# Attention and feed-forward kernel: another order of the work on the first four tiles, and the scales' floor by an instruction with two tensors

## The chip, the cores and the metric

The kernel runs on one core of one Trainium2 chip. The metric is the device time of one execution in microseconds (us), lower is better. A core has five engines with an instruction queue each: TensorE (PE in the profile, its weight loads PEld), VectorE (DVE), ScalarE (ACT), GpSimd (POOL) and SyncE (SP, which only issues transfers here). Each engine takes its own instructions in program order and waits on semaphores that others raise.

## What is computed

```python
x = x + xattn(layernorm(x), ctx, ctx)      # x, ctx: 32 x 64 x 512, fp32
x = x + ffn(layernorm(x))

# xattn, for each batch entry: q = Wq x + bq, k = Wk ctx + bk, v = Wv ctx + bv  (64 x 64 weights)
#   8 heads of 64 columns: p = softmax(q k^T / 8), out = Wo (p v) + bo
# ffn: gate, up: 512 x 1792, down: 1792 x 512, int32 weights, one zero and one scale for 128 rows each
#   w = (imatrix - zero) * scale
#   y = (silu(x @ gate) * (x @ up)) @ down
```

## The kernel before

The 32 x 64 rows of `x` are 16 tiles of 128 rows (two batch entries each), and 4 chunks of 4 tiles. For each tile the attention has a fixed series of steps, and every engine has a few of them:

- `stats(0, t)` (VectorE), `rstd` (GpSimd, a power of -0.5), `shift` (VectorE) and `norm1` (ScalarE) make the first layer norm.
- `project(t)` (TensorE, line 663) makes q and k of both entries in PSUM; `take_qk(t, 0)` and `take_qk(t, 1)` (VectorE, L943) add the biases and put them into SBUF. Their buffer `qkT` is single, so `take_qk(t+1)` waits for `score(t)`.
- `score(t)` (TensorE, L673) makes the scores. `most(t)` (VectorE, L957) takes the largest one of each row, `less_max(t)` (L963) subtracts it, `power_of(t)` (ScalarE, L526) takes the exponential, `invert(t)` (VectorE, L970 and L973) makes the sum and its reciprocal, and `weigh(t)` (GpSimd, L391) multiplies by it.
- `values(t)` (TensorE, L681) and `take_v(t)` (ScalarE, L521) make v; `mix(t)` (TensorE, L692) applies Wo to the weights p, `take_a(t)` (ScalarE, L535) takes the result, `apply(t)` (TensorE, L703) multiplies by v, and `residual(t)` (VectorE, L982) adds it to `x`.
- `stats(1, t)`, `rstd`, `shift(1, t)`, `norm2(t)`, then `turn_x(t)` (TensorE, L722): the second layer norm, transposed. `take_x` (ScalarE, L544) and `rest_x` (VectorE, L989) split it into a high and a low part in `xT`. For the fourth tile this is done in halves (L616, L885, L621, L1119).

`PRE` is 4: the first four tiles go through all of this ahead of the loop over the feed-forward. I call this part the front; its order is written out by hand, as one list of calls for each engine. PSUM banks, `xn`, `v_sb` and `e_sb` are shared by neighbouring tiles, so a list sets which tile waits for which. `stir(n)` (TensorE, L796) is filler: n multiplications of the identity whose result nobody reads.

After the front comes a loop of places `q`, in which TensorE makes the gate and up products (`gate_up`, L764 and L766) and the down products (`down`, L777 and L778) of a chunk while the attention of the next tiles is put between them. `project`, `values` and `score` of the fifth tile (t = 4) reach into the loop: `project(4)` is still in the front, its `take_qk(4, 0)` and `take_qk(4, 1)` stand at the end of VectorE's front, and `score(4)` comes after the first `gate_up`. The start of the first `gate_up` waits for the low part of the fourth tile's first half (`s_lastlo`).

Two kinds of work stand beside the attention in the front. The int32 weights come in pieces of 512 KB with their zeros (SyncE waits for each of the first five pairs before it issues the next), and GpSimd's `less_zeros(k)` (L409) subtracts the zeros of a piece, `convert(k)` (ScalarE, L548) makes it a float. In the loop VectorE does both for every second piece (L997). And the scales are prepared once: ScalarE copies them from PSUM (L583, L584), VectorE's `prepare` (L1003 to L1010) takes the absolute values, their largest one in each column, a floor from it (`fl`) and a comparison with it, GpSimd's `raised` (L434) spreads the floor, VectorE's `divide` (L1016, L1019) puts in the scales that are above it and inverts, and GpSimd's `ratios` (L439 to L442) makes the ratios with which ScalarE rescales.

## Time and profile before

| | |
|---|---|
| time, median of 3 runs | 434.78 us (434.33 to 435.92) |
| the profiled execution's own time | 434.57 us |
| its span, first to last instruction | 432.8 us |
| mean granted TensorE clock in the span | 0.996 of 2.4 GHz |
| busy: PE, PEld, DVE, ACT, POOL | 410.4, 317.9, 330.4, 330.5, 265.8 us |
| start of the first `gate_up` (end of the front) | 45.45 us |
| PE busy in 0 to 46 us | 38.5 of 46 us, much of it filler |
| HBM read, written | 30.56 MB, 4.19 MB |

The span is one execution recorded by the hardware profiler; all times of instructions below count from its start. The profiled execution took 0.2 us less than the median. Busy time of an engine is not the same as being needed: each engine waits for others in the front, and TensorE fills its waits with `stir`.

### The profile page before, as it was taken

Reading aid. Unit: us, or ns where it says so; the run is one execution under the profiler, and the core shown is the slowest. Engines: PE = TensorE matmul, PEld = TensorE weight load, DVE = VectorE, ACT = ScalarE, POOL = GpSimd, SP = SyncE. Lnnn points to the kernel's source line nnn. Section 1 sums busy time; section 2 is a strip of 40 time slices with the busy share of each in tenths; the row PEclk is TensorE's granted clock in tenths of the full one; section 3 lists DMA queues with packets and bytes.
Section 4 is the critical chain, followed back from the end, with each engine's and each line's share of the span. In section 5 each row is a group of like instructions: output and inputs, shape, how many; then the busy total and the mean of one; then the engine's idle time right before and its main releaser. Section 6 shows DMA issues by size and latency. Waiting matters only on the chain.

```text
span 432.8 us, 10751 instructions
## 1 busy us (share of the span) xinstructions
PE 410.4 (95%) x4228; PEld 317.9 (73%) x4228; DVE 330.4 (76%) x582; ACT 330.5 (76%) x540; POOL 265.8 (61%) x264
## 2 busy tenths in 40 slices
PE   7878988999988999999999999999999999999994
PEld 5655666777856777777777878677877888888872
DVE  4778666998878778788887777787887667667676
ACT  2438898897877788687778888687888998988970
POOL 3335797899588654665473954755566555555561
PEclk9899999999999999999999999999999999999999
DMA  7677746966742000002010000000000000001003
GB/s 255 190 230 259 279 147 226 300 204 209 241 121 69 2 11 16 26 2 76 12 39 26 2 0 27 27 2 26 26 27 0 2 1 9 17 24 50 1 1 97
DMA packets 26792, 35.44 MB, mean 82 GB/s; under 512 B 1870, under 2 KB 18422, under 8 KB 26742
## 3 DMA queue, kind: packets, MB, share of 16 engines
q1 hardware_dynamic: 26434, 34.71, 24.5%
q8 instruction: 33, 0.54, 0.5%
q14 instruction: 17, 0.14, 0.1%
q10 hardware_dynamic: 244, 0.05, 0.1%
q0 software_dynamic: 64, 0.00, 0.0%
HBM read 30.56 MB, written 4.19 MB: 80 GB/s over the span
## 4 chain that ended last, share of the span: by engine, by line
PE 73%; DVE 9%; issue 6%; POOL 6%; ACT 4%; DMA 1%; POOLq 0%; SPq 0%; DVEq 0%; ACTq 0%
PE banks L764 20%; PE banks L766 19%; PE banks L777 10%; PE banks L778 9%; PE banks L663 4%; DVE yT L1039 2%; PE banks L703 2%; ACT banks L555 2%; PE banks L692 2%; PE banks L673 2%; PE banks L681 2%; POOL t_sb L416 1%; DVE st L925 1%; PE banks L722 1%; DVE qkT L943 1%
## 5 line engine op out<-in xcount | busy, mean ns | idle before, releaser
L555 ACT ACTIVATE banks<-banks,ratio 128x512 f32<-128x512 f32 x336 | 207.8, 664 | 34.9 <-PE banks L766 25.4
L1039 DVE SCALAR_TENSOR_TENSOR yT<-banks,sd,yT 128x512 f32<-128x512 f32 x208 | 154.1, 746 | 48.8 <-PE banks L778 48.1
L764 PE MATMUL banks<-xT,wgu 128*128 128x512 f32 x448 | 182.2, 407 | 5.2 <-DVE t_sb L1024 2.5
L766 PE MATMUL banks<-xT,wgu 128*128 128x512 f32 x448 | 175.1, 391 | 0.0
L416 POOL TENSOR_TENSOR t_sb<-t_sb,u_sb 128x512 f32<-128x512 f32 x56 | 72.7, 1298 | 63.1 <-DVE t_sb L1024 63.0
L764 PEld LDWEIGHTS banks<-xT,wgu 128*128 128x128 f32 x448 | 84.1, 188 | 27.6 <-issue 3.7
L766 PEld LDWEIGHTS banks<-xT,wgu 128*128 128x128 f32 x448 | 84.3, 188 | 15.2
L777 PE MATMUL banks<-hr,wd 128*128 128x512 f32 x224 | 89.3, 399 | 4.2 <-DVE yT L1039 2.3
L778 PE MATMUL banks<-hr,wd 128*128 128x512 f32 x224 | 87.5, 390 | 0.0
L429 POOL TENSOR_TENSOR hr<-t_sb,hr 128x512 fp32r<-128x512 f32 x56 | 73.1, 1305 | 5.1 <-ACT hr L577 0.7
L777 PEld LDWEIGHTS banks<-hr,wd 128*128 128x128 f32 x224 | 42.0, 188 | 19.3 <-DVE yT L1039 9.5
L1024 DVE SCALAR_TENSOR_TENSOR t_sb<-t_sb,banks 128x512 f32<-128x512 f32 x56 | 38.3, 684 | 20.5 <-ACT t_sb L563 20.4
L563 ACT ACTIVATE t_sb<-banks,half_g 128x512 f32<-128x512 f32 x56 | 38.9, 694 | 13.7 <-PE banks L766 10.1
L778 PEld LDWEIGHTS banks<-hr,wd 128*128 128x128 f32 x224 | 42.1, 188 | 8.1
L385 POOL TENSOR_TENSOR rs<-ve,power 128x1 f32<-128x1 f32 x32 | 18.9, 592 | 35.2 <-DVE ve L929 35.1
L571 ACT ACTIVATE u_sb<-banks,last_u 128x512 f32<-128x512 f32 x56 | 38.5, 688 | 0.9 <-POOL t_sb L416 0.9
L425 POOL CAST hr<-t_sb 128x512 fp32r<-128x512 f32 x55 | 35.0, 636 | 6.1 <-PE banks L778 3.0
L391 POOL TENSOR_TENSOR e_sb<-e_sb,ri 128x512 f32<-128x512 f32 x16 | 17.0, 1065 | 28.5 <-DVE ri L973 28.5
L925 DVE BATCH_NORM_STATS2 st<-x_sb 128x6 f32<-128x512 f32 x32 | 21.8, 681 | 3.6 <-DMA x_sb<-in_x 3.6
L521 ACT ACTIVATE v_sb<-banks,bvo 128x512 f32<-128x512 f32 x16 | 11.0, 687 | 15.8 <-PE banks L681 15.4
L409 POOL TENSOR_TENSOR wgu_in<-wgu_in,z_in 128x1024 int32<-128x1024 int32 x9 | 21.5, 2393 | 1.1 <-DMA z_in<-in_L_ffn_gate_z 1.1
L943 DVE TENSOR_TENSOR qkT<-banks,bqk 128x512 f32<-128x512 f32 x32 | 21.5, 679 | 0.8 <-PE banks L663 0.8
(93 smaller groups left out, 383.9 us busy)
## 6 DMA issues: line engine op xcount, KB each, us to landing
x_sb<-in_x SPq DMA_DIRECT2D x16, 256.0 KB, 5.2
out<-x_sb SPq DMA_DIRECT2D x16, 256.0 KB, 2.1
wgu_in<-in_L_ffn_gate_w SPq DMA_DIRECT2D x7, 512.0 KB, 5.7
z_in<-in_L_ffn_gate_z SPq DMA_DIRECT2D x7, 512.0 KB, 5.4
wgu_in<-in_L_ffn_up_w SPq DMA_DIRECT2D x7, 512.0 KB, 5.5
z_in<-in_L_ffn_up_z SPq DMA_DIRECT2D x7, 512.0 KB, 5.0
wd_in<-in_L_ffn_down_w SPq DMA_DIRECT2D x7, 512.0 KB, 5.3
z_in<-in_L_ffn_down_z SPq DMA_DIRECT2D x7, 512.0 KB, 4.6
```

The costliest lines, as they stand in the source:

```text
L416: pool.tensor_tensor(h, h, u_sb[:, :], ALU.mult).then_inc(s_h, 1)
L425: pool.tensor_copy(hr[:, n % 2, 0, :], t_sb[:, n % 2, :]).then_inc(s_hi, 1)
L429: pool.tensor_tensor(hr[:, n % 2, 1, :], t_sb[:, n % 2, :], hr[:, n % 2, 0, :].bitcast(F32), ALU.subtract).then_inc(s_lo, 1)
L555: act.activation(banks[:, bank, :], banks[:, bank, :], ACT.Copy, scale=ratio[:, m, g, it:it + 1]).then_inc(done[n % 2], 1)
L563: act.activation(t_sb[:, n % 2, :], banks[:, G_BANK[n % 2], :], ACT.Tanh, scale=half_g[:, it:it + 1]).then_inc(s_tanh, 1)
L571: act.activation(u_sb[:, :], banks[:, U_BANK[n % 2], :], ACT.Copy, scale=last_u[:, it:it + 1]).then_inc(s_uf, 1)
L764: pe.matmul(banks[:, bank, :], w, xT[:, c % 2, 0, g, :], start=g == 0, stop=False, skip_group_check=True)
L766: pe.matmul(banks[:, bank, :], w, xT[:, c % 2, 1, g, :], start=False, stop=True, skip_group_check=True).then_inc(full[n % 2], 1)
L777: pe.matmul(bank, w, hr[:, n % 2, 0, :], start=True, stop=False)
L778: pe.matmul(bank, w, hr[:, n % 2, 1, :], start=False, stop=True).then_inc(s_full, 1)
L1024: dve.scalar_tensor_tensor(t, t, 1.0, banks[:, G_BANK[n % 2], :], ALU.add, ALU.mult).then_inc(s_gt, 1)
L1039: dve.scalar_tensor_tensor(y, bank, sd[:, it, b:b + 1], y, ALU.mult, ALU.add).then_inc(s_free, 1)
```

## The change

Nothing of what is computed changes except the way in which one small step is written. The change has these parts:

1. VectorE: `take_qk(1, 0)` and `take_qk(1, 1)` stand together in front of `invert(0)`, and so do those of the third tile in front of the second tile's sum; `shift(0, t)` comes right after its statistics; `prepare()` stands behind `take_qk(2, 1)`, `most(1)` and `less_max(1)` ahead of it; `residual(2)` stands ahead of `invert(3)`, `divide()` moves up in front of `residual(2)`; both `take_qk(4, .)` stand at the very end. `rest_x(0)` comes after `invert(3)`.
2. TensorE: `score(1)`, `score(2)` and `score(3)` come sooner, ahead of `project(2)`, `project(3)` and `values(2)`; `turn_x(1)` moves behind `mix(3)`; the fillers are cut up otherwise.
3. ScalarE and GpSimd lists are put in a matching order: the copies of the scales after `take_v(0)`, `raised()` after `weigh(2)`, and `less_zeros(2)` before `weigh(3)` instead of behind it.
4. `invert(t)` waits for `weigh(t-1)` for t = 1, 2 and 3, not for 3 alone (the buffer of reciprocals is single).
5. The floor `max(fl * 2^-30, 1e-37)` is a `scalar_tensor_tensor` with a second tensor `tiny` (a column of 1e-37 that GpSimd sets) in place of a `tensor_scalar` with two constants.

```diff
+            pool.memset(tiny[:, :], 1e-37).then_inc(s_id, 1)
...
             weigh(0)
             less_zeros(0)
-            raised()
             weigh(1)
             rstd(1, 0)
             less_zeros(1)
             weigh(2)
+            raised()
             rstd(1, 1)
+            less_zeros(2)
             weigh(3)
-            less_zeros(2)
...
             mm.then_inc(s_tr2, 1)
-            stir(2)
+            stir(3)
+            pe.wait_ge(s_sub, 1)
+            score(1)
             pe.wait_ge(s_qk, 4)
             project(2)
             pe.wait_ge(s_wT, 3)
             values(0)
-            stir(1)
-            pe.wait_ge(s_sub, 1)
-            score(1)
+            stir(2)
...
             apply(2)
-            stir(2)
+            stir(3)
             pe.wait_ge(s_x1, 3)
             values(3)
-            turn_x(1)
-            stir(1)
+            stir(4)
             pe.wait_ge(s_v, 4)
             mix(3)
+            turn_x(1)
+            apply(3)
...
-                if t == PRE - 1:
+                if 1 <= t < PRE:
                     dve.wait_ge(s_p, t)
...
-                dve.tensor_scalar(fl[:, :, :], fl[:, :, :], 2.0 ** -30, 1e-37, ALU.mult, ALU.max).then_inc(s_pr, 1)
+                dve.wait_ge(s_id, 5)
+                dve.scalar_tensor_tensor(fl[:, :, :], fl[:, :, :], 2.0 ** -30,
+                                         tiny[:, :].unsqueeze(2).to_broadcast([P, 2, NI]), ALU.mult, ALU.max).then_inc(s_pr, 1)
...
             take_qk(1, 0)
+            take_qk(1, 1)
+            invert(0)
             take_w(1)
             dve.tensor_copy(bvo[:, :], banks[:, 7, 4 * D:4 * D + 2]).then_inc(s_wT, 1)
-            invert(0)
-            take_qk(1, 1)
-            shift(0, 3)
+            most(1)
+            take_qk(2, 0)
+            less_max(1)
+            take_qk(2, 1)
             prepare()
-            most(1)
             dve.wait_ge(s_wT, 3)
             residual(0)
-            less_max(1)
-            take_qk(2, 0)
-            take_qk(2, 1)
             invert(1)
...
+            shift(1, 0)
             residual(1)
             invert(2)
             most(3)
-            shift(1, 0)
+            stats(1, 1)
             less_max(3)
-            stats(1, 1)
+            divide()
+            residual(2)
             invert(3)
+            rest_x(0)
             shift(1, 1)
-            residual(2)
-            rest_x(0)
             stats(1, 2)
             stats(0, 4)
+            shift(1, 2)
             rest_x(1)
-            shift(1, 2)
             residual(3)
             shift(0, 4)
             stats(1, 3)
-            divide()
             shift(1, 3)
             rest_x(2)
-            take_qk(4, 0)
             for h in range(2):
...
+            take_qk(4, 0)
             take_qk(4, 1)
```

VectorE's queue from the second tile's q and k to the first tile's residual, before (`qkT` is q and k, `mx` the largest scores, `sm` and `ri` the sum and its reciprocal, `e_sb` the scores less their maximum, `nm` the mean's shift, `ab`, `fl`, `big` the scales' preparation, `x_sb<-banks` the residual):

```order
L943 TENSOR_TENSOR qkT<-banks,bqk 128x512
L1056 COPY wT<-banks 128x128
L1077 COPY bvo<-banks 128x2
L970 TENSOR_REDUCE sm<-e_sb 128x8
L973 RECIPROCAL ri<-sm 128x8
L943 TENSOR_TENSOR qkT<-banks,bqk 128x512
L933 TENSOR_SCALAR nm<-mv,rs 128x1
L1003 SCALAR_TENSOR_TENSOR ab<-sg 128x112
L1005 TENSOR_REDUCE fl<-ab 128x28
L1008 TENSOR_SCALAR fl<-fl 128x28
L1010 TENSOR_TENSOR big<-ab,fl 128x112
L957 TENSOR_REDUCE mx<-banks 128x8
```

and in the changed kernel:

```order
L941 TENSOR_TENSOR qkT<-banks,bqk 128x512 x2
L968 TENSOR_REDUCE sm<-e_sb 128x8
L971 RECIPROCAL ri<-sm 128x8
L1056 COPY wT<-banks 128x128
L1080 COPY bvo<-banks 128x2
L955 TENSOR_REDUCE mx<-banks 128x8
L941 TENSOR_TENSOR qkT<-banks,bqk 128x512
L961 TENSOR_TENSOR e_sb<-banks,mx 128x512
L941 TENSOR_TENSOR qkT<-banks,bqk 128x512
L1001 SCALAR_TENSOR_TENSOR ab<-sg 128x112
L1003 TENSOR_REDUCE fl<-ab 128x28
L1007 SCALAR_TENSOR_TENSOR fl<-fl,tiny 128x28
```

The second tile's q and k are now two instructions in a row, its maximum and its subtraction stand in front of the scales' preparation instead of behind it (the subtraction stood even behind the residual), and the third tile's q and k too.

TensorE's queue after the second tile's projections, before (`wT,xn` and `wT,ctx_pre` are projections, `ctx_pre,wT` values, `qkT` scores, `wT,e_sb` the mix, `ident` filler):

```order
L796 MATMUL banks<-ident 128x256
L663 MATMUL banks<-wT,xn 64x64 x16
L663 MATMUL banks<-wT,ctx_pre 64x64 x16
L681 MATMUL banks<-ctx_pre,wT 64x256 x4
L796 MATMUL banks<-ident 128x128
L673 MATMUL banks<-qkT 64x64 x16
L692 MATMUL banks<-wT,e_sb 64x64 x16
```

and in the changed kernel:

```order
L798 MATMUL banks<-ident 128x384
L675 MATMUL banks<-qkT 64x64 x16
L665 MATMUL banks<-wT,xn 64x64 x16
L665 MATMUL banks<-wT,ctx_pre 64x64 x16
L683 MATMUL banks<-ctx_pre,wT 64x256 x4
L798 MATMUL banks<-ident 128x256
L694 MATMUL banks<-wT,e_sb 64x64 x16
```

The second tile's scores moved from behind the third tile's projections and the first tile's values to the place in front of them.

VectorE's queue at the fourth tile's sum, in the changed kernel (`sp_` and `ab<-sp_` are `divide`; before, the residual stood behind the sum and `divide` 16 rows further on):

```order
L961 TENSOR_TENSOR e_sb<-banks,mx 128x512
L1016 COPY_PREDICATED sp_<-big,sg 128x112
L1019 RECIPROCAL ab<-sp_ 128x112
L980 SCALAR_TENSOR_TENSOR x_sb<-banks,bvo,x_sb 128x512
L968 TENSOR_REDUCE sm<-e_sb 128x8
L971 RECIPROCAL ri<-sm 128x8
L987 TENSOR_TENSOR xT<-banks,xT 128x4x128
```

The third tile's residual now precedes the fourth tile's sum, and the two instructions of `divide` precede both.

## Rows read from the trace of the kernel before

**Rows 1.** Busy time by stretch: PE, PEld, DVE, ACT, POOL, granted clock, DMA share, GB/s
```profile
200.00:300.00 100.00, 99.34 (x1076) 77.19 (x1078) 78.17 (x139) 78.21 (x130) 58.70 (x63) 1.00 0.07 23
```

**Rows 2.** Timeline, PE in the front: start, duration, engine, line, what, [idle before <- releaser]
```profile
15.96 0.73 PE L663 MATMUL banks<-wT,xn 64*64 64x64 f32 x32 [1.29 <-DVE qkT L943]
...
19.06 1.06 PE L673 MATMUL banks<-qkT 64*64 64x64 f32 x32
...
23.12 0.66 PE L681 MATMUL banks<-ctx_pre,wT 64*64 64x256 f32 x8 [0.31 <-DVE x_sb L982]
...
24.91 0.69 PE L663 MATMUL banks<-wT,xn 64*64 64x64 f32 x32 [0.71 <-DVE qkT L943]
...
27.60 0.33 PE L673 MATMUL banks<-qkT 64*64 64x64 f32 x4 [1.07 <-issue]
...
28.49 0.69 PE L692 MATMUL banks<-wT,e_sb 64*64 64x64 f32 x32
...
33.50 0.83 PE L692 MATMUL banks<-wT,e_sb 64*64 64x64 f32 x32 [0.54 <-POOL e_sb L391]
...
38.11 0.69 PE L692 MATMUL banks<-wT,e_sb 64*64 64x64 f32 x32
...
45.45 0.47 PE L764 MATMUL banks<-xT,wgu 128*128 128x512 f32 x1
```

**Rows 3.** Timeline, DVE in the front
```profile
13.56 0.69 DVE L943 TENSOR_TENSOR qkT<-banks,bqk 128x512 f32<-128x512 f32 x1 [0.25 <-PE banks L663]
...
14.43 0.67 DVE L970 TENSOR_REDUCE sm<-e_sb 128x8 f32<-128x512 f32 x1
...
22.32 0.75 DVE L982 SCALAR_TENSOR_TENSOR x_sb<-banks,bvo,x_sb 128x512 f32<-128x512 f32 x1 [1.43 <-PE banks L703]
22.98 0.68 DVE L963 TENSOR_TENSOR e_sb<-banks,mx 128x512 f32<-128x512 f32 x1
```

**Rows 4.** Timeline, ACT in the front: the first tile's v
```profile
18.52 0.69 ACT L521 ACTIVATE v_sb<-banks,bvo 128x512 f32<-128x512 f32 x1 [4.37 <-PE banks L681]
```

**Rows 5.** Busy time by stretch of 1 us, columns as in rows 1
```profile
17.00:18.00 1.00, 1.00 (x30) 0.58 (x24) 0.99 (x1) 0.00 (x0) 1.00 (x1) 0.50 1.08 380
```

**Rows 6.** Timeline, POOL and DVE side by side, at two places
```profile
15.42 1.04 POOL L391 TENSOR_TENSOR e_sb<-e_sb,ri 128x512 f32<-128x512 f32 x1 [3.03 <-DVE ri L973]
...
15.95 0.64 DVE L1003 SCALAR_TENSOR_TENSOR ab<-sg 128x112 f32<-128x112 f32 x1
...
16.43 2.37 POOL L409 TENSOR_TENSOR wgu_in<-wgu_in,z_in 128x1024 int32<-128x1024 int32 x1
...
17.01 1.84 DVE L1008 TENSOR_SCALAR fl<-fl 128x28 f32<-128x28 f32 x1
...
125.56 2.40 POOL L409 TENSOR_TENSOR wd_in<-wd_in,z_in 128x1024 int32<-128x1024 int32 x1
...
126.39 2.13 DVE L997 TENSOR_TENSOR wgu<-wgu_in,z_in 128x512 fp32r<-128x512 int32 x1
```

**Rows 7.** Timeline, POOL and DVE at `divide`
```profile
42.24 0.55 POOL L385 TENSOR_TENSOR rs<-ve,power 128x1 f32<-128x1 f32 x1 [2.39 <-DVE ve L929]
42.41 0.85 DVE L1019 RECIPROCAL ab<-sp_ 128x112 f32<-128x112 f32 x1
...
43.18 0.12 DVE L933 TENSOR_SCALAR nm<-mv,rs 128x1 f32<-128x1 f32 x1
```

**Rows 8.** Timeline, DVE, POOL and PE early in the loop
```profile
50.82 0.68 DVE L997 TENSOR_TENSOR wgu<-wgu_in,z_in 128x512 fp32r<-128x512 int32 x1
...
50.85 1.28 POOL L396 TENSOR_SCALAR xn<-x_sb,rs,nm 128x512 f32<-128x512 f32 x1
...
52.38 0.69 PE L663 MATMUL banks<-wT,xn 64*64 64x64 f32 x32
```

**Rows 9.** The zeros' transfers, 30 to 60 us: one issue, and their times to landing
```profile
39.24 0.51 SPq L328 DMA_DIRECT2D z_in<-in_L_ffn_up_z  x1
...
DMA to landing us min/median/max: 4.3/4.9/8.0
```

53 lines of the change are left out of this document (25 added, 28 removed).

## The prediction

> **What bounds the kernel now.** I first read busy time by stretch. From 200 to 300 us TensorE works 99.34 of 100 us [rows 1]: the loop has no room, and what the front takes is added to it. So the question is how much sooner the first gate product starts, now at 45.45 us [rows 2], and how much of that the loop hands on. All work that the change touches lies in front of it.
>
> Next the timeline of TensorE and VectorE in the front. The reader should see a relay: mix(1) starts at 28.49, mix(2) at 33.50, mix(3) at 38.11, the first gate product at 45.45 [rows 2]. From each mix to the next runs one chain over four engines (mix, aT, apply, residual, sum, weigh, mix), and its length, 5.01 and 4.61 us, is latency and not work. Ahead of mix(1) the chain is not so tight, and there the time is lost: TensorE stands 1.29 us in front of project(2) for the second half of the second tile's q and k, which VectorE makes only after the first tile's sum; score(1) comes at 19.06 although its input is there at about 15.9 [rows 2]; and the subtraction of its maximum comes at 22.98, behind the first residual at 22.32, which waited 1.43 us for TensorE [rows 3].
>
> **The change, part by part.** A VectorE instruction of 128x512 lets the next one start 0.60 us after its own start, and ends 0.68 after it; the sum and the reciprocal take 0.83 together (from 14.43 to 15.26; the q and k behind them end 0.65 later, just ahead of TensorE's 15.96) [rows 2, 3].
>
> *Up to mix(1).* The first half of q and k starts at 13.56 as before [rows 3], since nothing before it is faster. The second ends at 13.56 + 0.60 + 0.69 = 14.85, so score(1) starts at 14.9, 4.1 us sooner. Scores and projections of a tile take about 1.6 us (24.91 to 26.53, where the gap begins with four matmuls left) [rows 2], values 0.66: all is done at 17.1. v(0) then takes 0.69 [rows 4], so mix(0) starts at 17.9, and, with the 2.05 us that mix, aT and apply take in a row, apply(0) ends near 20.0.
> VectorE's arm: 13.56 + 1.2 (q, k) + 0.83 (sum of tile 0) = 15.6; + 0.26 (two small copies) = 15.85; maximum, q and k, subtraction, q and k, 4 x 0.60 and 0.2 of waits = 18.5. Now comes prepare. Its first instruction reads two SBUF tensors. GpSimd's weigh(0) starts 0.35 later than before, at 15.77, and takes 1.04, and less_zeros(0) then takes 2.37 [rows 6]: until 19.17. I let the first instruction end 0.13 after that, as it did before (below), then 0.38 + 0.2 + 0.3 for the other three: 20.2. Residual(0) 0.66 (22.32 to 22.98), sum and reciprocal 0.91, weigh 1.04 and two handovers of 0.07: 22.95. mix(1) could start at 23.0.
> TensorE's arm: score(2) and project(3) follow apply(0) and end at 21.4, values(1) + 0.66, v(1) + 0.69, handovers 0.1: 22.9. But inside score(2) there is a gap of 1.07 us that ends at 27.60, whose reason is "issue" [rows 2]: no semaphore held TensorE, and I read it as a wait for its own instructions. As many instructions into the program, the changed kernel stands in values(1), so I put the same gap there: 23.9. I take mix(1) at 23.9 against 28.49: **4.6 us gained**; without the gap 5.5.
>
> *mix(1) to mix(2).* The order of the relay is unchanged, 5.0 us. *mix(2) to mix(3):* before, the sum of tile 3 stood ahead of residual(2), 4.61; now it stands behind it, as in the previous leg, which took 5.01. Hence **-0.4**. Divide's two instructions (0.3, and 0.85 [rows 7]) lie between less_max(3) and residual(2), where VectorE has about 1.1 us to spare, since apply(2) ends about 2.1 after mix(2). They cost nothing; were that cover gone they would cost 1.1. less_zeros(2) now runs ahead of weigh(3): rstd 0.55 + 2.37 against VectorE's 3.3 us from the statistics to the reciprocal, also covered, by 0.3 us.
>
> *mix(3) to the first gate product*, 7.34. Divide is gone from here: GpSimd's rstd ended at 42.79 and the shift that waits for it started at 43.18, behind the reciprocal [rows 7]: **+0.4**. But turn_x(1) now stands behind mix(3), by addition of its steps its low part (VectorE) ends about 2.45 after mix(3) started, and residual(3), which could start at 2.15 (30.65 - 28.49 in an earlier leg), is behind it: **-0.3**. 4.6 - 0.4 + 0.4 - 0.3 = 4.3: first gate product at 45.45 - 4.3, about **41.2 us**.
>
> *The loop.* take_qk(4, 0) stood where VectorE waited anyway; now it stands behind the halves that release the gate product, and the fifth tile's next statistics come 0.60 later relative to it. They feed GpSimd's norm, which ended at 52.13, and TensorE's project(5) at 52.38 [rows 8]: 0.25 of slack, so 0.35 is lost, 0.6 at most. I take 0.6, since one gap in one trace is thin cover.
>
> *The floor.* L1008 takes 1.84 us for 28 elements. It started at 17.01 and ended 0.05 after GpSimd's less_zeros(0) (16.43 + 2.37); it waited for GpSimd [rows 6]. Who sees the new instruction might book 1.6 us. But instructions with two SBUF tensors wait as well: L1003 took 0.64 and ended 0.13 after weigh(0), and an L997 of 0.68 us took 2.13 beside GpSimd's L409 at 125.56, and ended 0.56 after it [rows 6]. Bounds for the new form: 0.2 with GpSimd at rest, 2.4 at worst behind a fresh L409. Both forms stand where less_zeros(0) is over, so I take 0.2 for either, and book nothing for the edit.
> The Trainium skill, "GPSIMD Engine Reference", section 1 (Specifications), says that GpSimd shares its SBUF interfaces with VectorE, for instructions in a two-port mode or with two SBUF inputs. By that rule the two-tensor form waits just as the old one did, and the rows agree; without it the sum would be up to 1.6 us better, if the preparation were on the path.
>
> *The rest.* The longer waits of invert(1) and invert(2) for weigh(0) and weigh(1), done 4 us earlier, cost nothing. Fillers: they fill waits; up to 0.3 each way.
>
> *The clock.* In 17 to 18 us the granted clock is 0.50, the level of 1.2 GHz [rows 5]; it is low for some three us, after TensorE had waited 1.29 us at 15.96 [rows 2]. In the changed kernel TensorE has hardly a gap from 13 to 17, so I take 2.4 GHz. Were it low again, score, mix and values would cost about 0.9 more.
>
> **Sum.** 4.3 - 0.6 = 3.7 against the profiled execution's own 434.57: 430.9. The median is 0.2 above that execution, so 431.1.
>
> **The rivals.**
> - *The clock still falls.* Against it speaks the denser queue. 431.1 + 0.9 = 432.0. Chance 0.12.
> - *TensorE's own gap falls beside the path.* It hangs on when instructions arrive. 431.1 - 0.9 = 430.2. Chance 0.10.
> - *Divide is held by GpSimd.* Its first instruction reads two SBUF tensors and starts within 0.1 us of less_zeros(2); if that comes first, VectorE stands 2.4 us, residual(2) and the sum behind it. 1.1 are covered, and weigh(3) moves with them: 1.3 to 1.65 lost, 432.6. For it: rows 6. Against: where VectorE was first, GpSimd was the one to wait, as the L396 that started 0.03 behind an L997 and took 1.28 [rows 8]. Chance 0.12.
> - *The data are late.* The loop's zeros are issued at times that do not move (39.24; landing 4.3 to 8.0 later) [rows 9] and read at 50.82 [rows 8], now 46.6. At 47.2 they would be 0.6 late, mostly covered; with several such waits 2 us are given back: 433.1. Chance 0.08.
> - *The order does not do what it says*, as some wait holds score(1) where it was: 434.8. Chance 0.04.
> - *Slower.* TensorE's work in the front falls to 1.2 GHz for most of it. At that level mix and apply (0.7 each) take twice as long: 1.4 more in each of three legs, some 2.5 in the last one with its projections and transposes, 0.9 ahead of them: +7, 438. It decides once more than half of the front is low. For it: rows 5. Against: the clock recovered after the one low stretch, and the later gaps are no longer than 1.1. Chance 0.04.
>
> **How the numbers follow.** The forecast itself, within 0.8, has 0.50. A measurement of this kernel can tell about 0.5%, 2.2 us, so faster is anything under 432.6: most of the forecast, all of the second rival, most of the first, half of the third: 0.73. Same 0.23, slower 0.04. The range goes from 429.9 (no gap, loop loss 0.35) to 433.6, past divide held and late data.
>
> **What would show it.** First gate product near 41.2; score(1) near 14.9; mix(1), mix(2), mix(3) near 23.9, 28.9, 33.9; L1007 at 0.2 with L1001 at about 0.8; granted clock 1.00 from 13 on; L1016 under 0.5. I am wrong if mix(1) starts after 25, if residual(2) follows a long L1016, or if the gate product comes 4 us sooner and the end does not.

## The result, and the profile after

The changed kernel took 436.87 us (median of 16 runs, 435.07 to 438.52) where the kernel before took 434.84 (16 runs, 433.99 to 436.48) beside it: a ratio of 1.0033, 95% interval [1.0019, 1.0047], by which it is 1.4 us slower (the two medians are 2.0 apart). Forecast were 431.1 us and a gain. By the bound of 0.5% this is no change; by its interval it is a small loss, and nothing of the 3.7 us arrived. The profiled execution of the changed kernel has a span of 435.3 us (before 432.8) and a mean granted clock of 0.993.

The loop is as full as it was, so what is missing is missing ahead of it. Busy time by stretch, PE, PEld, DVE, ACT, POOL, granted clock, DMA share, GB/s, in the changed kernel (answers to [rows 1]), and a stretch further on that is spoken of below:

```profile
200.00:300.00 100.00, 99.33 (x1050) 77.39 (x1049) 78.16 (x140) 78.79 (x132) 59.01 (x62) 1.00 0.07 23
```
```profile
130.00:135.00 5.00, 3.63 (x11) 2.42 (x12) 4.93 (x11) 1.81 (x3) 3.38 (x4) 0.76 0.34 107
```

The timeline of TensorE in the front of the changed kernel (answers to [rows 2]; L675 is scores, L694 the mix, L798 filler, L766 the gate product):

```profile
17.15 1.14 PE L675 MATMUL banks<-qkT 64*64 64x64 f32 x32
...
21.34 0.69 PE L694 MATMUL banks<-wT,e_sb 64*64 64x64 f32 x32 [0.25 <-ACT v_sb L523]
...
27.28 0.70 PE L798 MATMUL banks<-ident 128*128 128x256 f32 x2 [2.01 <-issue]
27.91 0.69 PE L694 MATMUL banks<-wT,e_sb 64*64 64x64 f32 x32
...
32.92 0.46 PE L694 MATMUL banks<-wT,e_sb 64*64 64x64 f32 x15 [0.32 <-POOL e_sb L393]
33.78 0.47 PE L694 MATMUL banks<-wT,e_sb 64*64 64x64 f32 x17 [0.41 <-issue]
...
38.56 0.69 PE L694 MATMUL banks<-wT,e_sb 64*64 64x64 f32 x32 [0.32 <-POOL e_sb L393]
...
46.02 0.47 PE L766 MATMUL banks<-xT,wgu 128*128 128x512 f32 x1
```

The relay does start sooner: the second tile's scores come at 17.15 (19.06 before; 14.9 was forecast). But mix(1) is at 27.91 (28.49), and in front of it TensorE stands 2.01 us with "issue" as the reason: nothing that the profile shows held it. That is the gap that was 1.07 us inside score(2) before, and it ends at almost the same time, 27.28 against 27.60. Behind it the legs are 5.01 and 5.64 us (5.01 and 4.61 before), and the last one 7.46 (7.34), so the first gate product comes at 46.02, 0.57 us *later* than before, not 4.3 sooner.

VectorE's side in the changed kernel (L955 maximum, L941 q and k, L1001 to L1010 the scales' preparation, L980 the residual, L1016 and L1019 `divide`; answers to [rows 3, 7]):

```profile
14.78 1.29 DVE L941 TENSOR_TENSOR qkT<-banks,bqk 128x512 f32<-128x512 f32 x2 [0.29 <-PE banks L665]
...
18.35 0.69 DVE L955 TENSOR_REDUCE mx<-banks 128x8 f32<-128x512 f32 x1 [1.23 <-PE banks L675]
...
22.54 0.19 DVE L1007 SCALAR_TENSOR_TENSOR fl<-fl,tiny 128x28 f32<-128x28 f32 x1
...
23.58 0.75 DVE L980 SCALAR_TENSOR_TENSOR x_sb<-banks,bvo,x_sb 128x512 f32<-128x512 f32 x1 [0.55 <-PE banks L705]
...
33.74 0.27 DVE L1016 COPY_PREDICATED sp_<-big,sg 128x112 f32<-128x112 int32 x1
...
41.11 0.74 DVE L980 SCALAR_TENSOR_TENSOR x_sb<-banks,bvo,x_sb 128x512 f32<-128x512 f32 x1
```

Residual(0) ends at 24.3, so the sum, the weights p and with them mix(1) could have followed at about 26.4 (0.91 and 1.04 us and two handovers on); TensorE was the one that came late. The new floor takes 0.19 us and `divide` runs without a wait. This execution also had a slow start: q and k come at 14.78, the third tile's data came 1.7 us later than in the profile of before, and 32 records of 64x64 products take 1.08 to 1.14 us up to 19.8 and 0.65 to 0.70 behind it, although the profile gives the granted clock as 1.00 there. So a second execution follows below.

### The profile page after: what moved, and what is told of

The parts are those of the page before. It is cut to its first block, busy times and chain, and to the rows that moved or that the text cites. A ratio compares the mean times of both kernels' runs of the same rounds, so it can differ in the third digit from the quotient of the medians.

```text
span 435.3 us, 10739 instructions
## 1 busy us (share of the span) xinstructions
PE 412.4 (95%) x4220; PEld 318.4 (73%) x4220; DVE 329.2 (76%) x582; ACT 331.0 (76%) x540; POOL 265.7 (61%) x265
## 4 chain that ended last, share of the span: by engine, by line
PE 70%; DVE 9%; issue 8%; POOL 6%; ACT 5%; DMA 1%; SPq 1%; POOLq 0%; DVEq 0%; ACTq 0%
PE banks L766 19%; PE banks L768 18%; PE banks L779 10%; PE banks L780 9%; PE banks L665 3%; DVE yT L1039 3%; PE banks L705 2%; PE banks L694 2%; ACT banks L557 2%; PE banks L675 2%; PE banks L683 2%; POOL t_sb L418 1%; DMA x_sb<-in_x 1%; DVE st L923 1%; POOL wgu_in L411 1%
## 5 line engine op out<-in xcount | busy, mean ns | idle before, releaser
L766 PE MATMUL banks<-xT,wgu 128*128 128x512 f32 x448 | 182.6, 408 | 4.6 <-DVE t_sb L1024 2.5
L766 PEld LDWEIGHTS banks<-xT,wgu 128*128 128x128 f32 x448 | 84.4, 188 | 26.5 <-issue 3.7
L1024 DVE SCALAR_TENSOR_TENSOR t_sb<-t_sb,banks 128x512 f32<-128x512 f32 x56 | 38.3, 685 | 20.6 <-ACT t_sb L565 20.4
L923 DVE BATCH_NORM_STATS2 st<-x_sb 128x6 f32<-128x512 f32 x32 | 21.8, 681 | 5.1 <-DMA x_sb<-in_x 5.1
L941 DVE TENSOR_TENSOR qkT<-banks,bqk 128x512 f32<-128x512 f32 x32 | 21.5, 682 | 1.3 <-PE banks L665 1.3
```

What stands on the lines that cost most here:

```text
L766: pe.matmul(banks[:, bank, :], w, xT[:, c % 2, 0, g, :], start=g == 0, stop=False, skip_group_check=True)
L1024: dve.scalar_tensor_tensor(t, t, 1.0, banks[:, G_BANK[n % 2], :], ALU.add, ALU.mult).then_inc(s_gt, 1)
```

## Theories

**Supply.** TensorE's own instructions come by transfer, as the page's table of DMA queues shows: a queue "instruction" with 33 packets and 0.54 MB, 16.4 KB each. If one packet is a block of instructions, and if it has to stand behind 0.5 MB weight pieces in the same 16 transfer engines, then the block with the instructions around the gap comes late for a reason that lies outside TensorE's work. By this theory TensorE could not pass that place before about 27 us in either kernel, and whatever the relay gained ahead of it was waited away.

**Rivals.** The gap is a length of its own (1 to 2 us at that operation) and the rest was lost in the relay; the new fourth-tile order costs what the front gained; the new floor or the prediction's last term (the loop's start) does.

Three readings speak for supply. First, how many instructions stand ahead of the gap. Windows from 0 to a point inside the gap, before and then changed (columns as above; the counts in brackets are what matters):

```profile
0.00:26.50 26.50, 21.81 (x474) 15.59 (x474) 17.65 (x43) 8.80 (x14) 8.81 (x18) 0.94 0.70 226
```
```profile
0.00:25.25 25.25, 21.94 (x474) 15.51 (x474) 14.96 (x41) 7.31 (x12) 7.72 (x18) 1.00 0.74 236
```

474 products and 474 weight loads in both, although the 475th is inside score(2) in one and filler ahead of mix(1) in the other. Counted with all of TensorE's own records, the gap begins at record 961, and the other gaps with the reason "issue" in this study's fronts begin at 705, 1217 or 1729, at distances of 256.

Second, when the block comes. The changed kernel's transfers from 25 to 26 us, in 40 slices, and the two queues:

```profile
DMA  6202900200000000000000000000000000000000
...
q8 instruction: 1, 0.02, 6.1%
q1 hardware_dynamic: 13, 0.01, 4.0%
```

The block goes at 25.1, as the last 13 packets of the weights drain, and TensorE goes on at 27.28, 2.2 us later. And third, SyncE's issues in the changed kernel, each of which waits for the pair before it to land:

```profile
19.65 0.37 SPq L316 DMA_DIRECT2D wgu_in<-in_L_ffn_gate_w  x1
...
25.05 0.37 SPq L316 DMA_DIRECT2D wgu_in<-in_L_ffn_up_w  x1
...
31.68 0.37 SPq L316 DMA_DIRECT2D wd_in<-in_L_ffn_down_w  x1
```

The blocks start at 19.49, 25.11 and 31.43 us; before at 19.06, 25.24 and 30.37, with pairs landed at 19.4, 25.3 and 32.0. They start mostly as the weights run down. (The last of before is 1.6 us early, so it need not be the landing itself that frees a block.)

But they follow TensorE too, and that is the half of the mechanism that the theory above leaves out. Up to record 1473, in every one of the sixteen profiles, each block starts 0.4 to 7.1 us *after* TensorE has passed the 256-record boundary before the one that it serves. For the block behind record 961 that boundary is record 705: TensorE passes it at 21.60 us before and 22.87 changed, the block starts 3.6 and 2.2 us later, and TensorE passes record 961 another 2.4 and 2.2 us later. (These times come from counting TensorE's records in the traces, some of which may be missing.) So a block seems to be asked for about when the one before it is entered, and the weights that are already queued then set how long it stands. The Trainium skill, "Runtime: NRT & Kernel Launch", section Instruction fetch mechanics, has the blocks (16 KiB, 256 instructions, the next one fetched by the sequencer's own queue while the current one is executed), and the traces agree: one start for each boundary passed. It calls the cost of crossing a block mostly hidden, and here it is 2.01 us, and up to 3.65 below.

## The experiments

Milestones of each profiled execution, in us from the span's start. A wait is given as its length and, in brackets, its end; all of them have the reason "issue". The last column has when TensorE passes record 705 and when the block behind record 961 then starts.

| kernel | score(1) | mix(1) | mix(2) | mix(3) | gate | waits at 705, 961 | block for 961 |
|---|---|---|---|---|---|---|---|
| before | 19.06 | 28.49 | 33.50 | 38.11 | 45.45 | -, 1.07 (27.60) | 21.60, 25.24 |
| changed | 17.15 | 27.91 | 32.92 | 38.56 | 46.02 | -, 2.01 (27.28) | 22.87, 25.11 |
| changed, second execution | 14.48 | 27.56 | 33.95 | 38.97 | 46.42 | 1.98 (21.16), 2.84 (26.41) | 21.16, 24.10 |
| changed, weights late | 14.04 | 23.59 | 28.60 | 33.60 | 44.50 | 0.36 (19.36), 1.19 (22.96) | 19.36, 20.60 |
| changed, more instructions | 18.08 | 29.75 | 35.92 | 40.92 | 49.25 | 1.57 (21.23), 1.85 (27.51) | 21.23, 25.02 |
| changed, 4th tile as before | 15.49 | 28.46 | 34.40 | 39.95 | 48.10 | 1.16 (21.35), 3.65 (27.41) | 21.35, 25.07 |
| changed, piece 2 paced | 14.91 | 26.11 | 31.12 | 36.22 | 43.66 | 1.98 (21.60), 1.47 (25.48) | 21.60, 22.84 |
| changed, pieces 1 and 2 paced | 15.22 | 24.16 | 29.17 | 34.17 | 41.63 | -, 1.45 (23.53) | 19.68, 21.30 |

### The changed kernel again

No edit: a second execution.

> The changed kernel once more, for a second profile. Supply theory (TensorE runs out of its own instructions, which reach it in blocks and queue behind the weight transfers): the gap in front of mix(1) comes again at the same instruction, 1.5 to 2.2 us long, ends at 27.2 to 27.8 us, and smaller ones come again in mix(2) and score(4). Clock theory (TensorE stayed at 1.2 GHz until 20 us, and that took the gain): the low clock comes again; if it rises at 13 us this time, mix(1) should start 2 us sooner by this theory, and no sooner by the supply theory.

One run, 436.43 us; TensorE in the front:

```profile
14.48 0.69 PE L675 MATMUL banks<-qkT 64*64 64x64 f32 x32 [0.75 <-DVE qkT L941]
...
21.16 0.52 PE L705 MATMUL banks<-v_sb,aT 64*64 64x64 f32 x20 [1.98 <-issue]
...
26.41 1.22 PE L798 MATMUL banks<-ident 128*128 128x256 f32 x2 [2.84 <-issue]
27.56 1.13 PE L694 MATMUL banks<-wT,e_sb 64*64 64x64 f32 x32
```
```profile
28.00:32.00 4.00, 3.98 (x98) 3.02 (x94) 1.02 (x2) 1.81 (x3) 0.00 (x0) 0.50 0.88 284
```

With data in time the second tile's scores come at 14.48, as forecast (14.9), 2.7 us sooner than in the first profile, and mix(1) at 27.56, only 0.35 sooner. What the relay gained more was waited away, in two gaps of 4.8 us together. After the second one the granted clock fell to 0.50, the level of 1.2 GHz, from 26.2 to 33.0 us, and the leg from mix(1) to mix(2) took 6.39 us in place of 5.01. So the wait costs twice: it swallows the gain, and slow work follows it. The supply theory had 1.5 to 2.2 us for the gap, an end at 27.2 to 27.8, and smaller ones in mix(2) and score(4); the place was right, the length and the end were not, and the smaller ones did not come. Nor do "as the pair runs down" and these blocks agree: they start at 24.1 and 28.2, 3.3 and 5 us ahead of the landings (27.4 and 33.1). Passing the boundary explains them better. TensorE passed record 705 at 21.16, when one piece of weights had been issued (20.89) and its zeros had not (21.30), and the block started 2.9 us on, while that piece was landing (23.85 to 24.73) and ahead of its zeros (25.4 to 27.3); it passed 961 at 26.41 with the transfer engines nearly idle, and the next block started 1.75 us on. That is read off one profile and was not tried by a run of its own.

### Weights late, in both kernels

SyncE issues the pieces from the second one on only after mix(3), so that the transfer engines are free in the relay; what works on those pieces (`less_zeros` and `convert` of 1 and 2) moves behind it. The end of the run means nothing; the front does.

```diff
             for k in range(PACED):
+                if k == 1:
+                    load_x(PRE)
+                    load_ctx(PRE)
+                    sync.wait_ge(s_bM, PRE)
                 load_w(k)
```

> The changed kernel with the weight pieces 1 to 4 transferred, and the zeros of 1 and 2 subtracted and converted, only after mix(3); the end of the front is then late and counts for nothing, only what comes up to mix(3) does. Supply theory: no gap over 0.4 us whose reason is issue, mix(1) at 23.5 to 25.5, mix(2) 5.0 later, mix(3) 5.0 after that. Clock theory: the clock is as before the same, mix(1) not before 26.5.

> The same edit to the kernel before. Supply theory: the gap of 1.07 us in score(2) is gone, mix(1) at 27.3 instead of 28.5, so 2 to 3.5 us behind the changed kernel with this edit. Clock theory: mix(1) at 28.3 or later, less than 1.5 us behind it.

Changed kernel, TensorE:

```profile
22.96 0.70 PE L802 MATMUL banks<-ident 128*128 128x256 f32 x2 [1.19 <-issue]
23.59 0.69 PE L698 MATMUL banks<-wT,e_sb 64*64 64x64 f32 x32
...
28.60 0.69 PE L698 MATMUL banks<-wT,e_sb 64*64 64x64 f32 x32 [0.32 <-POOL e_sb L397]
...
33.60 0.69 PE L698 MATMUL banks<-wT,e_sb 64*64 64x64 f32 x32 [0.33 <-POOL e_sb L397]
```

Forecast were 23.9, 28.9 and 33.9: the relay's arithmetic holds to 0.3 us once the weights are out of the way. The expectation of no gap over 0.4 us failed, though: 1.19 us are left at the same record, with no weights on the way. TensorE passes record 705 at 19.36, the block starts at 20.60 and TensorE goes on at 22.96, so 256 records took 3.6 us here with the transfer engines free, where TensorE by itself is through with them in 2.0 us. (GpSimd and ScalarE have less to do there too, so this run shows that the relay can run so, and not by itself why it did not.) The kernel before, treated alike, had mix(1) at 28.22, mix(2) at 33.23 and mix(3) at 37.89, with no gap in its front: it is 4.6 us behind at mix(1) and, by the shorter leg, 4.3 at mix(3). Taking its own 1.07 us away brought mix(1) forward by 0.27 only, but this execution began late (granted clock 0.50 from 8.1 to 21.8 us, score(1) at 19.90 for 19.06): from score(1) to mix(1) it took 8.32 us for 9.43, 1.1 less. So the gap lay on the path there too, and with the waits on SyncE below, where it is gone as well, mix(1) of the kernel before comes at 27.55 and 27.45. The late start makes the 4.6 us of this pair too large; with both pieces paced the two kernels are 3.3 us apart at mix(1) and 2.8 at the gate (44.45 and 41.63). The blocks of the changed kernel now start at 12.06, 17.2, 20.6 and 24.1 us.

### More instructions in front

The first filler, 2 products of 128x512 and 128x256, becomes 32 of 64x64. Nothing is reordered, but everything behind stands some 60 recorded products further on in TensorE's stream.

```diff
             pe.wait_ge(s_id, 2)
-            stir(6)
+            for _ in range(32):
+                pe.matmul(blocks(RING_BANK + 1)[0:D, 0, 0:D], ident[0:D, 0:D], ident[0:D, 0:D], start=True, stop=True)
```

> The first six filler columns (2 matmuls of 128x512 and 128x256, 2.93 us in the changed kernel's profile) are given as 32 matmuls of 64x64, about as long together: nothing later is moved in the order, but every later instruction of TensorE stands some 60 matmul records further back in its stream. Supply theory (a block of 256 instructions of TensorE arrives at a time set by the weight transfers, about 21.5 and 27.0 us, and TensorE cannot pass the same place in the stream before): the waits for nothing shown are found some 60 matmul records earlier in the program, the first in or ahead of mix(0), not in apply(0), the second inside the fourth tile's projections, not ahead of mix(1), and each still ends near 21.5 and 27.0. The work behind the second place (rest of project(3), values(1), filler, some 2 us) then comes after 27.0, so mix(1) starts at 28.7 to 29.3, where the changed kernel had 27.56 and 27.91, and the gate begins 1.0 to 1.5 us later, near 47.5. Rival (the wait is a length of its own or belongs to the operation at which it stands, the filler ahead of mix(1)): the place does not move, mix(1) stays at 27.3 to 28.0 and the gate at 46.0 to 46.5. Second rival (no relation to the stream: noise of one execution): no wait over 1 us at all, mix(1) near 24 to 25.

```profile
21.23 0.34 PE L665 MATMUL banks<-wT,ctx_pre 64*64 64x64 f32 x5 [1.57 <-issue]
22.87 0.69 PE L694 MATMUL banks<-wT,e_sb 64*64 64x64 f32 x32 [0.23 <-ACT v_sb L523]
...
27.51 0.51 PE L665 MATMUL banks<-wT,xn 64*64 64x64 f32 x19 [1.85 <-issue]
29.75 0.70 PE L694 MATMUL banks<-wT,e_sb 64*64 64x64 f32 x32
...
32.76 0.27 PE L705 MATMUL banks<-v_sb,aT 64*64 64x64 f32 x1 [0.91 <-issue]
```
```profile
0.00:25.60 25.60, 21.13 (x474) 17.39 (x475) 13.75 (x38) 7.31 (x12) 7.70 (x17) 1.00 0.73 233
0.00:27.50 27.50, 21.18 (x474) 17.39 (x475) 15.55 (x42) 7.31 (x12) 8.43 (x18) 1.00 0.71 225
```

One premise was wrong: the 32 small products took 6.98 us, not the 2.93 of the large ones, so the whole relay runs late (score(1) 18.08 where the second execution has 14.48). Mix(1) at 29.75 (expected 28.7 to 29.3) and the gate at 49.25 (expected near 47.5) therefore tell little. What stands is the place and the end of the waits. Again exactly 474 products stand ahead of the second one; it moved from the filler ahead of mix(1) back into the fourth tile's first projections; and it ends at 27.51, the first one at 21.23 (27.28 and 26.41, and 21.16, in the two executions of the changed kernel), although the relay ran 3.6 us late and TensorE stood elsewhere in it. A wait with a length of its own would have moved with the operation and with the delay, and been there in full. The first was expected at mix(0) and stood a little earlier, in the third tile's projections. One run gave 438.11 us.

### The fourth tile's part as before

VectorE's, GpSimd's, ScalarE's and TensorE's lists for the fourth tile as they were (`divide` behind the statistics, residual(2) behind `invert(3)`, `turn_x(1)` ahead of mix(3)); for VectorE:

```diff
             less_max(3)
-            divide()
-            residual(2)
             invert(3)
-            rest_x(0)
             shift(1, 1)
+            residual(2)
+            rest_x(0)
...
             stats(1, 3)
+            divide()
             shift(1, 3)
```

> The changed kernel with the fourth tile's part in the order of before: its sum ahead of residual(2), the division of the scales at the end, the third piece's zeros behind weigh(3), turn_x(1) ahead of mix(3). Leg theory (this order costs the relay up to 1 us): mix(2) to mix(3) 4.6 to 4.7 us instead of 5.64, and 0.6 to 1.0 us less in all, about 435.9. Supply theory alone: the same blocks arrive at the same times, so mix(3) at most 0.4 us sooner, and the time within 0.4 us of 436.9.

437.09 us, ratio 1.0034 [1.0009, 1.0058], the same as with the change whole. The last two legs were 5.55 and 8.15 us, not shorter. Its profile has the longest wait of all,

```profile
27.41 1.12 PE L798 MATMUL banks<-ident 128*128 128x256 f32 x2 [3.65 <-issue]
28.46 1.13 PE L694 MATMUL banks<-wT,e_sb 64*64 64x64 f32 x32
```

and slow work behind it (granted clock 0.50 from 27.6 to 31.0 us). That the new fourth-tile order costs the gain is refuted; whether it costs its 0.4 us this run cannot say.

### One wait on SyncE

If blocks start when a pair has drained, splitting a pair lets one in earlier. SyncE waits for weight piece 2 to land before it issues the zeros of piece 2; it waited for both together, one line later.

```diff
                 load_w(k)
+                if k in (2,):
+                    sync.wait_ge(s_w[k], 16)
                 load_zeros(k)
...
-                sync.wait_ge(s_w[k], 16)
+                if k not in (2,):
+                    sync.wait_ge(s_w[k], 16)
                 wait_zeros(sync, k)
```

> The changed kernel with one wait more on SyncE: the third weight piece has landed before its zeros are issued, so that the transfers in flight from 19.4 us on are half as many when TensorE's next block of instructions is asked for. Supply theory: that block starts at 22 to 23.5 us instead of 24.1 to 25.1, the gap ahead of mix(1) ends at 24.5 to 26 instead of 26.4 to 27.4, and the time falls by 0.5 to 2 us, to 435.0 to 436.4. If the blocks come at fixed times whatever the transfers: the gap ends where it did, and the time is the same or up to 2 us longer, since everything behind that piece lands 2 us later.

> The same wait in the kernel before. Supply theory: its gap of 1.07 us in score(2) goes, but there the relay itself is the bound, so at most 1 us is gained: 433.8 to 435.2. Fixed times: the gap stays, 434.8 to 437.

```profile
21.60 0.52 PE L708 MATMUL banks<-v_sb,aT 64*64 64x64 f32 x20 [1.98 <-issue]
...
25.48 0.70 PE L801 MATMUL banks<-ident 128*128 128x256 f32 x2 [1.47 <-issue]
26.11 0.69 PE L697 MATMUL banks<-wT,e_sb 64*64 64x64 f32 x32
...
43.66 0.47 PE L769 MATMUL banks<-xT,wgu 128*128 128x512 f32 x1
```

The block for record 961 starts at 22.84, just ahead of the zeros issued at 22.86 and 1.24 us after TensorE has passed record 705, as with the weights late (1.24), and TensorE goes on at 25.48. Start and end of the gap are as expected; the time is better than the 435.0 to 436.4 expected. The changed kernel takes **433.5 us, ratio 0.9961 [0.9939, 0.9982] to the kernel before**; the one wait turned its small loss into a small gain. The kernel before with the same wait: 434.82, 0.9986 [0.9965, 1.0008], no difference that shows. The kernel before does lose its gap and has its gate at 44.53, 0.9 us sooner, but 1.17 us of it go in a wait at record 1729. By the medians the new order is then worth 1.3 us, though the two intervals overlap; without the wait it was -1.4 by the ratio and -2.0 by the medians. Either ratio is within 0.5% of 1.

### Two waits, and the second supply

The same for pieces 1 and 2, in both kernels (`k in (1, 2)`).

> The changed kernel, with SyncE waiting for weight pieces 1 and 2 to land before it issues their zeros. Supply theory: block 2 of TensorE's instructions now starts between 16 and 18.5 (19.2 to 19.5 before) and block 3 no later than 22.8, so the first wait (1.98 us in apply(0)) falls under 0.5 and the second under 1.5; mix(1) at 24.3 to 25.5 (26.1 with piece 2 alone), gate near 42.5, time 432 to 433 and the ratio to the kernel before 0.992 to 0.996. Rival (TensorE's wait is bound to the amount in flight, not to the order of issue): no change against piece 2 alone, 433.5. A loss is possible where a weight piece comes too late for the loop's first rounding: then the first gate products, from 45 us on, have waits for weights of over 0.5 us.

> The kernel before with the same two waits on SyncE. Supply theory: the kernel before lost only 1.07 us to the supply, so it gains little: mix(1) at 27.3 to 27.6, the time 434.0 to 435.0, ratio 0.998 to 1.000; the difference between this and the changed kernel with the same two waits is then what the new order is worth with the instructions in time: 1.5 to 3 us. Rival (the pacing helps by something else, such as GpSimd's or the weights' order): it gains as much as the changed kernel does, 1.5 us or more.

```profile
23.53 0.70 PE L801 MATMUL banks<-ident 128*128 128x256 f32 x2 [1.45 <-issue]
24.16 0.69 PE L697 MATMUL banks<-wT,e_sb 64*64 64x64 f32 x32
...
29.17 0.69 PE L697 MATMUL banks<-wT,e_sb 64*64 64x64 f32 x32 [0.32 <-POOL e_sb L396]
...
34.17 0.69 PE L697 MATMUL banks<-wT,e_sb 64*64 64x64 f32 x32 [0.32 <-POOL e_sb L396]
...
41.63 0.47 PE L769 MATMUL banks<-xT,wgu 128*128 128x512 f32 x1
```

Blocks start at 17.0 and 21.3 (1.4 and 1.6 us after TensorE has passed the boundary before), the wait at 705 is gone, and the front is the forecast one: 24.16, 29.17, 34.17 and 41.63 against 23.9, 28.9, 33.9 and 41.2. And yet the time is 435.13, ratio 1.0005 [0.9987, 1.0022], where 432 to 433 were expected. The loop gives all back in one place, here GpSimd and TensorE:

```profile
49.23 2.34 POOL L414 TENSOR_TENSOR wgu_in<-wgu_in,z_in 128x1024 int32<-128x1024 int32 x1 [4.03 <-DMA z_in<-in_L_ffn_gate_z]
51.56 0.76 POOL L401 TENSOR_SCALAR xn<-x_sb,rs,nm 128x512 f32<-128x512 f32 x1
```
```profile
52.46 1.14 PE L668 MATMUL banks<-wT,xn 64*64 64x64 f32 x32 [4.16 <-POOL xn L401]
```

GpSimd stood 4.03 us for the zeros of a piece, the sixth tile's norm behind it in its queue, and TensorE's projection behind that; and then the granted clock is 0.50 from 51.9 to 58.7 us, which makes the loss larger than the wait (TensorE's products went from 4.2 us ahead of the kernel before to 1.75 behind). The added waits had put the issue of these zeros off from 37.2 to 43.0 us. The kernel before with both waits: 435.57, 1.0017 [0.9996, 1.0038], and a 2.54 us wait for the same norm.

The next two runs ask whether that was only the late issue. SyncE does not wait behind piece 4 any more, so that piece 5 is issued sooner, with both waits and with the one:

```diff
-                if k not in (1, 2):
+                if k not in (1, 2, 4):
                     sync.wait_ge(s_w[k], 16)
-                wait_zeros(sync, k)
+                if k < 4:
+                    wait_zeros(sync, k)
```

> The changed kernel with SyncE's waits for weight pieces 1 and 2 before their zeros, and without any wait behind piece 4, so that pieces 5 and on are issued some 6 us sooner (36.8 in place of 42.6). With the first two waits alone the gate began at 41.63, 3.8 us ahead of the kernel before, and then TensorE waited 4.06 us at 52.36 for a tile that GpSimd normalizes behind a piece whose zeros had been issued at 43.03 and landed at 49.2. Theory (both supplies come through the same 16 transfer engines, and the 3.8 us are lost only because the pieces were issued late): zeros of piece 5 land near 43 to 45, the wait at 52 goes to under 1, and the end comes 2 to 4 us sooner than with the two waits alone: 431.0 to 433.0, ratio to the kernel before 0.991 to 0.995. Rival (the total of bytes is the bound there: whoever starts the gate sooner waits for weights by as much, whatever the order of issue): the wait at 50 to 57 stays over 3 us and the time is 434 to 435.5. Second rival (pieces in flight hold back TensorE's blocks again): a new wait of over 1 us at records 1473 or 1729, near 38 to 43.

> The changed kernel with SyncE's wait for piece 2 alone (433.5 us) and without any wait behind piece 4. There the weights were not waited for by more than in the kernel before, so sooner pieces 5 and on bring nothing by themselves: 433.0 to 434.0. Rival (pieces in flight hold back TensorE's blocks): the 0.91 us at record 1729, in the fifth tile's score at 46.83, grows to 1.5 or more, and one at record 1473 appears: 434 to 435.5.

With both: 433.45 us, ratio 0.9960 [0.9936, 0.9985]; the wait for the norm shrank from 4.16 to under 0.3. Its profile has the gate at 43.36 (its front began at the low clock, score(1) at 15.94) and another wait, 1.95 us for VectorE's `t_sb` up to 55.42, so that its products from the 32nd on stood only 0.86 us ahead of the kernel before. With the one: 433.93, 0.9970 [0.9946, 0.9994], no better than without the edit, as expected. Late issue was the cause of the 4 us. The time expected with it, 431.0 to 433.0, was missed, and 431.1 was not reached by any version, and the three that gain end within 0.5 us of each other.

### The floor, and the loop's start

The floor's new form alone in the kernel before, and the old form in the changed kernel:

> The kernel before with the new form of the floor alone (the scalar_tensor_tensor with a second tensor in SBUF, its column of 1e-37 and the semaphore counts). If an instruction with two SBUF tensors waits for GpSimd as the old form does: it ends at the end of less_zeros(0) again, 1.5 to 2.4 us long, and the time is that of before. If it does not wait: 0.2 us long; the time still the same, since score(1) comes a microsecond after it.

> The changed kernel with the old form of the floor. GpSimd is at rest when the preparation runs here, if TensorE is as late as in the first profile, so I expect 0.15 to 0.25 us for it, and the time of the changed kernel. Where the relay is early (preparation at 18.5 to 20 us) it should wait for less_zeros(0), as its neighbour with two tensors does.

Kernel before with the new form, then changed kernel with the old one:

```profile
16.49 2.38 POOL L411 TENSOR_TENSOR wgu_in<-wgu_in,z_in 128x1024 int32<-128x1024 int32 x1
...
17.07 1.85 DVE L1011 SCALAR_TENSOR_TENSOR fl<-fl,tiny 128x28 f32<-128x28 f32 x1
```
```profile
16.82 2.36 POOL L411 TENSOR_TENSOR wgu_in<-wgu_in,z_in 128x1024 int32<-128x1024 int32 x1
...
18.55 0.77 DVE L1001 SCALAR_TENSOR_TENSOR ab<-sg 128x112 f32<-128x112 f32 x1
...
19.73 0.18 DVE L1007 TENSOR_SCALAR fl<-fl 128x28 f32<-128x28 f32 x1
```

In the place of before the new form takes 1.85 us, as the old one did (1.84, [rows 6]); with GpSimd at rest the old form takes 0.18 and the new one 0.19. The form is worth nothing at either place; only its place counts. One run each gave 437.12 and 437.84 us; the second had waits of 1.71 and 3.10 us at records 705 and 961 as the changed kernel has.

The first half of the fifth tile's q and k back ahead of the two last halves:

```diff
             rest_x(2)
+            take_qk(4, 0)
             for h in range(2):
...
-            take_qk(4, 0)
```

> Only the first half of the fifth tile's q and k (its eviction on VectorE) goes back ahead of the two last halves of the fourth tile's normalized tile. My prediction's step: this reordering starts the gate earlier and is worth 0.6 us in the loop's beginning; undone, the first halves are ready 0.6 to 0.7 us later, the gate begins 0.6 later than in the changed kernel for the same mix(3), that is mix(3) to first gate product 8.0 in place of 7.4, and the fifth tile's score starts no later than 1.5 us behind it. Rival (the gate waits for the last subtraction of the fourth tile through another engine): mix(3) to the gate 7.4 to 7.5 as now. In both the waits ahead of mix(1) and in score(5th tile) stay.

Mix(3) to the gate: 39.74 to 47.20, 7.46 us, as in the changed kernel (38.56 to 46.02). From the first gate product to the ninth the shift against the kernel before grows by 0.58 us with the edit and by 0.58 without it. The term is nothing in either direction. One run, 437.92 us.

## Why the prediction was wrong

It failed at one step, and the steps around it held.

- **The step that failed** is "I put the same gap there: 23.9". The gap was seen, read rightly as a wait for TensorE's own instructions, and rightly moved to the same count of instructions; it was then booked as a *length* (1.07 us) that travels along. It is no length but what is left of a delivery: the time at which TensorE passed the boundary before (record 705), plus 2.2 to 3.8 us until the block starts where weights are on the way, plus 2.2 to 2.5 us. That ends at 27.28 and 26.41 in the changed kernel and 27.60 before. Mix(1) came at 27.91 and 27.56, not 23.9. In the second execution the two waits, 4.8 us less the 1.07 booked, are all of the 3.7 us missing; in the first one 4.0 are missing, of which 2.3 had gone already in the slow start up to score(1) and 0.9 are the wait beyond the 1.07. That the two edited runs come so near 23.9 owes something to luck: with the weights away or paced the wait there is 1.19 and 1.45 us, close to the 1.07 that was booked for another reason. The rival "TensorE's own gap falls beside the path", at 0.10, came closest to the subject and pointed the wrong way. What I had in hand and did not draw on: the queue "instruction" on the page and the end of the gap, 2.4 us behind a packet at 25.24.
- **Up to mix(1), both arms: right.** Score(1) 14.48 (14.9); with the supply moved, mix(1) at 23.59 and 24.16 (23.9).
- **The legs: right where nothing else interferes.** 5.01 and 5.00 us with weights late or with two waits (5.0 and 5.0); in the kernel before with weights late 5.01 and 4.66, so the loss of 0.4 in the third leg is confirmed (it is 0.34 in this pair). In the changed kernel itself that leg took 5.64, of which 0.41 is one more wait of the same kind in mix(2).
- **The last leg: right in its two terms, 0.2 off in all.** It took 7.46 us (7.34 before) where +0.4 and -0.3 made 7.2. `Divide` gone brought its 0.4: the shift that makes the last norm comes 2.54 us behind residual(3) (43.65 less 41.11) against 2.91 (43.18 less 40.27). `turn_x(1)` cost as much: residual(3) at 2.55 behind mix(3) (41.11 less 38.56) against 2.16 (40.27 less 38.11). The -0.3 was 0.1 too small, and 0.1 more went between that shift and the gate (2.37 for 2.27).
- **Divide held by GpSimd: did not happen**, L1016 took 0.27; it started 0.07 us ahead of less_zeros(2) (33.74 and 33.81), a thin margin, but 0.07 us in each of the nine profiles that have both at this place. **The floor: right**, nothing, and by the mechanism named. **The loop's 0.6: wrong**, it is nothing.
- **Late data** (0.08) is a real mechanism: it took the whole gain as soon as the gate came 3.8 us sooner with late zeros. It was priced by one transfer, while the order of all pieces depends on what is waited for.
- **The clock: wrong by cause.** I looked for it where TensorE waits for data, ahead of mix(0). It fell behind the long waits for instructions instead, in the four profiles in which the wait at 961 was 2.8 us or more (mix(1) to mix(2) 5.9 to 6.4 us for 5.0). The price of 1.4 us a leg came out at 0.9 to 1.4, though mix does not take twice as long at the lower level (1.13 us for 0.69). In the loop it also fell at the end of a wait for data, the 4.16 us above.

Why a loss and not just nothing: in the first profile 0.57 us at the gate, then a wait of 1.00 us inside score(4) (record 1729; its block started at 46.72, that of before at 43.51), which leaves the products 1.05 us behind; and 1.5 us more from 104 to 146 us, where the granted clock is 0.50 from 132.6 to 136.0 (the 130 to 135 row above) and where one more wait for `yT` of 0.36 stands at 145.7. A shift of 0.34 to 0.38 us between 137 and 148 us is in all eleven profiles with the changed order and in none of the five with the order before, so it belongs to the order. The stretch of low clock is in five profiles with the changed order and in none with the order before; TensorE's waits ahead of it (0.84, 1.17 and 0.73 us) are nearly those of the kernel before (0.85, 1.05 and 0.73), where it did not fall. Why it falls there was not tried and stays open, as does what exactly a block waits for: that it is asked for at the boundary before it and stands behind the transfers queued by then fits the profiles, but no run here was made to tell it from other orders of service. Open is also by how much the changed kernel would gain with no wait at all at 961: the least that was reached is 1.19 us.

## What to carry to other kernels

A gap whose reason is "issue" is worth a count: how many instructions of that engine stand ahead of it, here and in a second kernel or at the next such gap. If the count is the same and the distances are one block, it is a point in the stream with an arrival time, and a faster way up to it is worth little until the arrival moves. Then look at two times: when the engine passed the boundary before it, and when the packet in the instruction queue started. Here, at record 705, they are 0.9 to 1.6 us apart where the weights were late or held back (2.3 in one such run), and 2.2 to 3.8 where a pair of them was queued. The difference is what other pacing won; no run got 256 records in less than 3.6 us across a wait. And where a front competes with bulk loads, the order and the waits of the issuing queue belong to the critical path: one wait on SyncE took the changed kernel from 1.4 us behind to 1.7 ahead by the ratios, and one wait more lost it all again.

## What was not expected of the hardware

- TensorE's instructions come in packets of 16.4 KB, 256 of its records apart. In the front of this kernel each starts after TensorE has passed the boundary before it: 1.1 to 1.2 us after it for three blocks of the changed kernel with late weights, when the transfer engines were idle, and mostly 2 to 4 us with a pair of 512 KB transfers queued. Where TensorE waited it went on 2.2 to 2.7 us behind that start. Waits from 0.4 to 3.65 us came of it.
- 32 products of 64x64 took 6.98 us at the start, where a 128x512 and a 128x256 product took 2.93; small filler is not cheap filler.
- VectorE's `TENSOR_SCALAR` with one tensor and two constants and its `SCALAR_TENSOR_TENSOR` with two tensors wait alike for a running GpSimd instruction: 1.84 and 1.85 us for 0.18 and 0.19 us of work.
